# Edge stage of a graph network: message split by ScalarE, lists in pairs of tiles, a VectorE loop of 24 slots; routing marks shared with GpSimd

## What is computed

```python
h   = layernorm(x)
a   = concat(h[src], h[dst], edge_weight) @ mW1 + mb1        # 103125 edges
m   = layernorm(silu(a)) * ln_g + ln_b
msg = silu(m @ mW2 + mb2)
agg = segment_sum(msg, src, 3125)                            # sums by source node
x   = x + h + silu(concat(h, agg) @ uW1 + ub1) @ uW2 + ub2
# then: layernorm, a gelu network of width 1024 on the rows with the
# highest router scores, and the residual
```

## Time and profile before

| | |
|---|---|
| median of 3 runs | 2228.12 us (2223.9 to 2229.85) |
| the profiled execution, its own time | 2226.9 us |
| its span | 2225.2 us |
| PE busy | 1961.5 us (88%), 11037 matmuls |
| DVE busy | 1736.7 us (78%), 4578 instructions |
| ACT busy | 1303.2 us (59%), 2495 |
| POOL busy | 1238.9 us (56%), 1177 |
| mean granted clock of PE | 0.946 |

### The profile page before, as it was taken

The page is one execution under the profiler, slowest core; times in us unless marked ns, Lnnn a source line. Parts: engine busy times, 40 slices in busy tenths (PEclk is TensorE's granted clock), DMA queues, the critical chain, the costliest instruction groups (busy, mean ns, idle before and its releaser), DMA issues. The chain is left out here.

```text
span 2225.2 us, 45282 instructions
## 1 busy us (share of the span) xinstructions
PE 1961.5 (88%) x11037; PEld 1681.0 (76%) x11038; DVE 1736.7 (78%) x4578; ACT 1303.2 (59%) x2495; POOL 1238.9 (56%) x1177
## 2 busy tenths in 40 slices
PE   3546765379999999999999999999999999799996
PEld 2324554268888888888888888888888888677775
DVE  5899999678877877877878878778778778345895
ACT  1112331257777777777777777777777777423321
POOL 8753222376666666666667666666666665503000
PEclk9987777579999999999999999999999999899998
DMA  3000000344333333333333333333333333000001
GB/s 126 0 0 21 26 26 20 100 123 147 97 92 94 96 96 91 94 97 92 94 94 97 92 93 97 91 94 96 95 93 93 97 92 80 25 17 8 22 1 58
DMA packets 107787, 165.05 MB, mean 74 GB/s; under 512 B 42141, under 2 KB 78330, under 8 KB 107485
## 3 DMA queue, kind: packets, MB, share of 16 engines
q0 software_dynamic: 42016, 111.40, 18.4%
q1 hardware_dynamic: 59822, 47.94, 6.8%
q10 hardware_dynamic: 5900, 5.08, 0.7%
HBM read 152.30 MB, written 11.65 MB: 74 GB/s over the span
## 5 line engine op out<-in xcount | busy, mean ns | idle before, releaser
L907 POOL DMA_INDIRECT g_rows<-b_table,idx_ring x792 | 764.4, 965 | 439.7 <-ACT act L957 281.4
L1038 PE MATMUL ps<-w2g,nT 128*128 128x256 f32 x3336 | 789.3, 379 | 0.0
L1038 PEld LDWEIGHTS ps<-w2g,nT 128*128 128x128 f32 x3336 | 601.6, 190 | 64.6
L946 ACT ACTIVATE normed<-act,shift,rstd_e 128x255 f32<-128x255 f32 x834 | 449.6, 588 | 13.0 <-DVE shift L1105 9.5
L1021 PE MATMUL psG<-msg,ohf 128*125 128x256 f32 x1668 | 427.9, 379 | 0.1
L962 ACT ACTIVATE nT<-psM 128x512 f32<-128x512 f32 x417 | 248.9, 597 | 263.1 <-PE psM L1030 263.1
L1072 DVE TENSOR_TENSOR agg<-psG,agg 125x256 f32 x834 | 347.7, 417 | 67.6 <-issue 13.4
L1012 PE MATMUL psH<-a_sb,ohT 128*128 x1668 | 349.1, 332 | 26.4 <-DVE ohT L1125 24.7
L1136 DVE TENSOR_TENSOR g_rows<-psH,g_rows 128x512 f32<-128x512 f32 x417 | 284.7, 683 | 65.3 <-PE psH L1012 57.4
L1142 DVE BATCH_NORM_STATS2 stat_e<-act 128x6 f32<-128x256 f32 x834 | 310.2, 413 | 2.2 <-ACT act L957 2.2
L1021 PEld LDWEIGHTS psG<-msg,ohf 128*125 128x125 f32 x1668 | 284.4, 187 | 24.6 <-issue 0.3
(11 more groups left out here) (193 smaller groups left out, 1975.1 us busy)
## 6 DMA issues: line engine op xcount, KB each, us to landing
loc_rows<-loc_d SPq DMA_DIRECT2D x139, 187.5 KB
g_rows<-b_table,idx_ring POOLq DMA_INDIRECT x792, 2.8
h_sb<-in_x SPq DMA_DIRECT2D x1, 3125.0 KB
b_table<-b_out SPq DMA_DIRECT2D x25, 125.0 KB
x_all<-in_x ACTq DMA_DIRECT2D x1, 3125.0 KB
out<-x_all SPq DMA_DIRECT2D x5, 625.0 KB
ohT<-ew_d SPq DMA_DIRECT2D x139, 9.0 KB
idx_ring<-rec SPq DMA_DIRECT2D x132, 3.0 KB
```

Of the source, the lines that this page charges most:

```text
L907: pool.indirect_dma_start(g_rows[:, j, n, :], None, b_table[:, :], bass.IndirectOffsetOnAxis(ap=which, axis=0)).then_inc(s_gather[j], 16)
L946: ins = nc.scalar.activation(normed[:, j % 2, n, 0:D - 1], act1[:, (j - 10) % RING, n, 0:D - 1], ACT.Identity, scale=rstd_e[:, g % 2, k:k ...
L1038: mm = pe.matmul(ps2[:, k, n, :], nT[:, k, n, q, :], w2g[:, q, :], start=(q == 0), stop=(q == 1))
```

## The change

1. **Lists in pairs.** Each block's list is padded to whole pairs of tiles (256), so both tiles of a slot belong to one block: `PAIRS` is 429, `TILES` 858. There is one block number a pair (`pair_block`), and `reg_load` loads 6 registers a body on TensorE.
2. **One sum a slot.** `psG` gathers both tiles in one accumulation, so VectorE adds once a slot and no longer waits for an addition before it in the slot.
3. **The message is split.** ScalarE writes silu(`ps2`) once as `high`, float32r in SBUF, and, after `act1`, a second time in float32 in place in `ps2`. VectorE subtracts, `low` = `ps2` - `high`, float32r, as the last instruction of its slot. TensorE sums `high` and `low` with `ohf` in float32r: four products of one record each for two of two. `psG` now waits for `s_low`, which VectorE sets in the slot before, and so does `ps2` before it overwrites its buffer.
4. **VectorE's order and loop.** The shift moves from the slot's start to just before `g_rows`, variance 4 and 5 one step later; the hardware loop of VectorE alone has `SPAN` = 4 bodies of 6 slots and loads 24 registers at its start, 17 times. The written-out bodies keep 6 slots and load 6.
5. **Routing.** Of the 13 columns of `or_` VectorE makes 10 and GpSimd 3 (`pool_columns`), into four buffers `orp` in memory of `f1` and `f2`. GpSimd does the first four supers' columns before the chain of `jump`, and those of super s+4 after scatter s. `route(s)` waits for both (`s_or`, `s_orp`).

```diff
-TILES = (EDGES + BLOCKS * (WIN - 1 + P - 1)) // P
-TILES += TILES % 2
-PAIRS = TILES // 2
+PAIRS = (EDGES + BLOCKS * (WIN - 1 + 2 * P - 1)) // (2 * P)
+TILES = 2 * PAIRS
...
+                def pool_columns(s):
+                    if s >= PRING:
+                        pool.wait_ge(s_win, s - PRING + 1)
+                    for k in range(PCOLS):
+                        c = s * COLS + COLS - PCOLS + k
+                        ins = pool.tensor_scalar(orp[s % PRING][:, k, :], iota_n[:, :], r_all[:, c:c + 1], None,
+                                                 ALU.is_equal)
+                    ins.then_inc(s_orp, 1)
+
+                pool.wait_ge(s_places, 1)
+                for s in range(PRING):
+                    pool_columns(s)
...
                     pool.indirect_dma_start(rec_d[:, :], bass.IndirectOffsetOnAxis(ap=dest[:, s:s + 1], axis=0),
                                             recw[:, s % 4, :, :].rearrange("p w n -> p (w n)"), None).then_inc(s_scat, 16)
+                    if s + PRING < SUPERS:
+                        pool_columns(s + PRING)
...
                     pe.wait_ge(s_or, s + 1)
+                    pe.wait_ge(s_orp, s + 1)
...
-                    V.tensor_tensor(or_[:, s % 2, :, :], r_all[:, own].unsqueeze(2).broadcast_to([P, COLS, P]),
-                                    iota_v.unsqueeze(1).broadcast_to([P, COLS, P]), ALU.is_equal)
+                    mine = slice(s * COLS, (s + 1) * COLS - PCOLS)
+                    V.tensor_tensor(or_[:, s % 2, :, :],
+                                    r_all[:, mine].unsqueeze(2).broadcast_to([P, COLS - PCOLS, P]),
+                                    iota_v.unsqueeze(1).broadcast_to([P, COLS - PCOLS, P]), ALU.is_equal)
...
-                        nc.scalar.activation(msg[:, (j - 13) % 2, :, :], ps2[:, (j - 13) % 2, :, :], ACT.Silu).then_inc(s_msg, 1)
+                        nc.scalar.activation(high[:, (j - 13) % 2, :, :], ps2[:, (j - 13) % 2, :, :], ACT.Silu).then_inc(s_high, 1)
...
+                    if has(t, 13):
+                        act.wait_ge(s_high, t - 12)
+                        nc.scalar.activation(ps2[:, (j - 13) % 2, :, :], ps2[:, (j - 13) % 2, :, :], ACT.Silu).then_inc(s_msg, 1)
...
-                        pe.wait_ge(s_msg, t - 13)
+                        pe.wait_ge(s_low, t - 13)
                         pe.wait_ge(s_ohf, t - 13)
-                        need(pe, s_agg, 2 * t - 30)
+                        need(pe, s_agg, t - 15)
                         for n in range(2):
-                            mm = pe.matmul(psG[0:NB, k, n, :], ohf[:, k, n, :], msg[:, k, n, :], start=True, stop=True)
+                            pe.matmul(psG[0:NB, k, 0:D], ohf[:, k, n, :], high[:, k, n, :], start=(n == 0), stop=False)
+                            mm = pe.matmul(psG[0:NB, k, 0:D], ohf[:, k, n, :], low[:, k, n, :], start=False, stop=(n == 1))
...
+                    if has(t, 13):
+                        dve.wait_ge(s_msg, t - 12)
+                        V.tensor_tensor(low[:, (j - 13) % 2, :, :], ps2[:, (j - 13) % 2, :, :], high[:, (j - 13) % 2, :, :],
+                                        ALU.subtract).then_inc(s_low, 1)
+
+                def bodies(d, count):
+                    prepare(d, count)
+                    for i in range(count):
+                        for j in range(RING):
+                            slot((d + i) * RING + j, d + i, j, i)
...
-                with dve.Fori(PEEL, DG) as d:
-                    body(d)
+                with dve.Fori(0, (DG - PEEL) // SPAN) as e:
+                    bodies(e * SPAN + PEEL, SPAN)
```

More of the change, by code:

```diff
@@ L35 @@
 EQR = 4
+PCOLS = 3
+PRING = 4
 LAST = 15
 PEEL = 3
+SPAN = 4
 H = 1024
@@ L42 @@
 MAGIC = 12582912.0
+assert (DG - PEEL) % SPAN == 0 and PAIRS % 3 == 0
 assert NODES == NB * BLOCKS and 0 < TAIL <= EC and (COLS * P + BLOCKS * (WIN - 1)) // WIN <= P
-MAGIC_W, MAGIC_P = MAGIC * WIN, MAGIC * P
+MAGIC_W, MAGIC_P = MAGIC * WIN, MAGIC * 2 * P
 def build(nc, io):
@@ L145, in build @@
             k16 = sb("k16", [P, 1], F32)
[L146 to L150, removed]
+            tid = sb("tid", [P, PG], F32)
+            tb_c = sb("tb_c", [P, PG, BLOCKS], F32)
+            tb_f = sb("tb_f", [P, PG], F32)
+            tb_i = sb("tb_i", [P, PG], I32)
+            or_ = sb("or_", [P, 2, COLS - PCOLS, P], BF16)
+            orp = [half[:, k * PCOLS * P // 2:(k + 1) * PCOLS * P // 2].bitcast(BF16).rearrange("p (t r) -> p t r", t=PCOLS)
+                   for half in (f1, f2) for k in range(PRING // 2)]
             oqv = sb("oqv", [P, 2, COLS, PLANES, WIN], BF16)
@@ L594, in route @@
                     for t in range(COLS):
-                        mm = pe.matmul(psK[:, s % 3, 0:PLANES * WIN], or_[:, s % 2, t, :],
+                        marks = or_[:, s % 2, t, :] if t < COLS - PCOLS else orp[s % PRING][:, t - COLS + PCOLS, :]
+                        mm = pe.matmul(psK[:, s % 3, 0:PLANES * WIN], marks,
                                        oqv[:, s % 2, t, :, :].rearrange("p n w -> p (n w)"),
@@ L707, in _ @@
                 link(V.tensor_scalar(r_all[:, :], f2[:, :], 1.0 / WIN, None, ALU.mult))
[L708 removed]
+                V.tensor_tensor(q_all[:, :], place[:, :], f2[:, :], ALU.subtract).then_inc(s_places, 1)
+                dve.wait_ge(s_places, 1)
                 def flat(ap):
@@ L796, in build @@
             ohT = sb("ohT", [P, RING, 2, P], F32R)
-            ohf = sb("ohf", [P, 2, 2, NB], F32)
+            ohf = sb("ohf", [P, 2, 2, NB], F32R)
             g_rows = sb("g_rows", [P, RING, 2, D], F32)
@@ L801, in build @@
             nT = sb("nT", [P, 2, 2, 2, P], F32)
-            msg = sb("msg", [P, 2, 2, D], F32)
+            high = sb("high", [P, 2, 2, D], F32R)
+            low = sb("low", [P, 2, 2, D], F32R)
             var_e = sb("var_e", [P, 2, 6], F32)
@@ L1116, in slot @@
                     variance(t, d, j, 3)
-                    if has(t, LAST):
-                        add(t, j, 1)
-                    variance(t, d, j, 4)
                     if has(t, 1):
@@ L1126, in slot @@
                                         node_col[0:NB, 0:1], None, ALU.is_equal).then_inc(s_ohT, 1)
-                    variance(t, d, j, 5)
+                    variance(t, d, j, 4)
                     if has(t, 13):
@@ L1131, in slot @@
                                         ALU.is_equal).then_inc(s_ohf, 1)
+                    variance(t, d, j, 5)
+                    shifts(t, d, j)
                     if has(t, 2):
@@ L1144, in slot @@
                         ins.then_inc(s_bn, 1)
+                    if has(t, 13):
[7 more added lines that the diff above has]
+                            slot((d + i) * RING + j, d + i, j, i)
                 def body(d):
-                    prepare(d)
-                    for j in range(RING):
-                        slot(d * RING + j, d, j)
+                    bodies(d, 1)
                 V.tensor_copy(nodes, iota_n[:, 1:NB + 1]).then_inc(s_nodes, 1)
```

68 lines of the change are left out of this document (37 added, 31 removed).

## The result

| | before | after |
|---|---|---|
| median | 2227.01 us (2223.9 to 2229.85, 4 runs) | 2244.89 us (2243.95 to 2250.37, 4 runs) |
| profiled execution: span | 2225.2 us | 2242.1 us |
| mean granted clock of PE | 0.946 | 0.925 |

The change made the kernel **0.9% slower**: ratio 1.0086, 95% interval 1.0064 to 1.0107. Forecast were 2178 us and a range of 2092 to 2238. The time lies outside it, on the side of the rival "the longer body must be fetched anew, and the clock falls at each turn", which had a chance of 0.09 and was priced at 2255.

A forecast was written before the change was run, and what follows sets the result against it. TensorE was taken to bound the edge loop and VectorE the routing; -26 us for the edge loop, -22 for routing and -1 for the end, against 2226.9, gave 2178 us, range 2092 to 2238.

The forecast's parts named there:

- the longer body must be fetched anew, and the clock falls at each turn: Rival for VectorE's loop turn: code fetch and half clock make the kernel slower, slot 3.53, total 2255 us; chance 0.09.
- TensorE's pace: Edge loop: four fp32r sums take 0.48 us for 0.86, so a slot falls from 3.508 to 3.13 us.
- ScalarE and VectorE: Edge loop: ScalarE needs 2.96 to 3.0 us a slot, VectorE 2.94, both under TensorE's 3.13.
- The load of 24 registers: VectorE's loop turn: the load takes 5.46 us, twice that of 12 registers, once in 24 slots.
- VectorE is set back by 5.36: VectorE's loop turn: lateness from the 5.46 us load, plus 0.17, less 0.27 hidden by `low`.
- TensorE stops for 4.2: Edge loop turn: TensorE waits at psG for 5.36 less 1.15, 4.2 us, or 0.175 us a slot.
- The free lateness of 1.15: Edge loop: VectorE may run 1.15 us late before TensorE has to wait for `low`.
- The clock term: Edge loop: half speed after TensorE's stops was taken to cost 0.04 us a slot.
- Routing: Routing stage: ten columns instead of 13 on VectorE, three on GpSimd; -22 us over 62 supers.
- The end: End of the edge stage: slots shrink a little from last psH to last root, -1 us; node stage unchanged.

The follow-up runs named there:

- span1_fp32: Changed kernel with VectorE's loop at 6 slots and the message split undone (one silu, fp32 sums, no `low`): 2245.0 us, ratio 1.0083 to the kernel before.
- span1_b: Changed kernel with VectorE's loop at 6 slots, loading 6 registers: 2121.7 us, ratio 0.9529 to the kernel before; without _b, on the different chip, 2315.4 us.
- span2_load24_b: Changed kernel with VectorE's loop at 12 slots, loading 24 registers, 12 never used: 2324.5 us, ratio 1.0448; without _b, on the different chip, 2454.8 us.
- span3_b: Changed kernel with VectorE's loop at 18 slots, loading 18 registers, and five groups of 6 ahead of it instead of three: 2181.9 us, ratio 0.9808.
- span2_b: Changed kernel with VectorE's loop at 12 slots, loading 12 registers: 2155.9 us, ratio 0.9682 to the kernel before.
- span1_mix: Changed kernel with VectorE's loop at 6 slots, two columns on GpSimd, and marks of supers 2 and 3 behind the jump chain: 2120.4 us, ratio 0.9522.
- cols0: Changed kernel with all 13 routing columns back on VectorE, none on GpSimd: 2432.0 us on the different chip, 2258.05 us on another.

## Why the prediction was wrong, step by step

The forecast gave a turn 5.2 us of TensorE's time, 4.2 for the stop and 1.0 for the clock; it measured 9.4. Two terms failed: the fetch of the body, put at nothing, and the clock behind the stop, put at a third of what it took.

- **TensorE's pace: right.** 3.11 between turns for a forecast 3.13; fp32r sums at psH's price. span1_fp32 confirms the 0.4 us.
- **ScalarE and VectorE: right.** (That a write to PSUM costs no more was assumed without a row.) The Silu that writes PSUM lasts 0.59 us like its kin, and ScalarE needs 2.98 a slot (2.96 to 3.0 forecast). VectorE's 2.94 is met by the 2.9 that span1_b's 19.1 us leave.
- **The load of 24 registers: right.** 5.37 measured, 5.46 taken. The Trainium skill (Runtime: NRT & Kernel Launch, Instruction fetch mechanics) gave about 200 ns a register; 24 registers show 224 each here.
- **"VectorE is set back by 5.36": right for the load, and the step that failed.** The sum had no term for the code. The forecast put the fetch into a rival, because the old body of 120 instruction records never was fetched again; the new one has 445 (records from branch to branch). The fetch costs VectorE 2.6 us of standing a turn (8.07 for span2_load24_b's 5.47) and, with the clock, 9.4 - 7.0 = 2.4 us of TensorE's time. The Trainium skill's rule (same section: a taken branch to code outside the two pages that the engine holds waits for a fetch) pointed to it, and the traces agree in kind: 445 records are read anew each time round, 335 (span3_b) are not. Where between the two it begins no run shows. The weight given to it, 0.09, was the mistake; nothing in the trace of before spoke against it for a body four times as long.
- **"TensorE stops for 4.2": right for the case it described.** 3.9 without a fetch. With it, 6.2. But it was released by `ohT` first (2.6 of the 3.9) and by `low` second; the forecast had TensorE stop at psG for `low` alone, and it stops already at psH. The free lateness of 1.15 fits TensorE's idle time (0.2 and 3.9 us for turns of 1.28 and 5.47, so 1.1 to 1.6 is free), but a turn costs more than its idle time: 0.5 and 2.0 for turns of 1.28 and 2.81, as if only 0.8 were free.
- **The clock term: failed too.** Taken were 0.04 a slot, 1 us a turn, on the ground that the loop is dense. Stops of 3.9 us together in a dense loop brought half speed behind every turn and cost 2.7 us (span2_load24_b), in the changed kernel 3.0. The row that showed it stood in the prediction (3.69 us idle, then half speed) and was discounted. A stop of 1.5 us (span2_b) brought none.
- By estimate, neither error alone turns the sign. Without the fetch a turn of 24 slots at 7.0 us gives 3.11 + 0.29 = 3.40, and 2245 - 416 x 0.10 = 2203; with the fetch and the forecast's clock, 9.4 - 2.0 = 7.4 gives about 2210. Both together lose 1%.
- **Routing: right in kind, -13 for -22.** VectorE's super fell as forecast; its last `or_` comes 18.8 us earlier (388.50 for 407.26), not 24. But three marks take 1.78 and not 1.65, the scatter that follows 1.05, so GpSimd's super is 3.05 and not 2.6, and it catches up little when it is late: its last scatter starts 10.9 us behind VectorE's last `or_`, for 6.0 before. Twelve marks of 10.1 us ahead of the jumps put the first scatter 3.5 us later.
- **The end: -1 forecast, about -6 measured.** Last psH start to the span's end is 334.4 before and 328.4 after. The adds follow the last root as forecast, but the wait between them and the node stage fell from 8.99 to 2.45 us in every kernel with the new lists. What ends that wait isn't resolved; that it is fixed was an assumption. The node stage took 1.9 us more here (285.9 for 284.0).

The profiled spans add up: first psH 13.2 us earlier, from the first to the last psH 1492.5 us for 1456.5 (428 slots for 416), the end 6.0 shorter: +16.8 for the measured 16.9.

## What to carry to other kernels

Price the turn of a hardware loop as three things: the register load by its length, the fetch of a body that doesn't stay, and the clock behind the stop they cause; a longer loop spreads a turn thinner only as long as none of the three is new. Look in the trace for packets of instructions at the turns, and compare one engine's longest standstill with the lateness that its consumer can let pass: in 12 slots, two loads of 1.4 us cost 0.8, one of 2.7 costs 2.0, one of 5.4 costs 7.0. Here the loop of 12 slots with two loads of 6 registers keeps all that the split gives: 2118 us, 4.8% under the kernel before, with the loop of 6 and span1_mix within 0.2% of it.

## What was not expected of the hardware

- **One chip is different.** On it the kernel before took 2272 and 2278 us for 2225 to 2227 on the others, and the kernels with the new stage lost far more: span1 2315 for 2122, span2_load24 2455 for 2324, cols0 2432 for 2258. In its traces TensorE's counts arrive in bunches 0.06 us apart, up to 2.5 us late, while the granted clock is full. Whether TensorE itself or only its counts are held up, and why, stays open; no trace of the kernel before was taken there. On that chip even the best version is 1.8% slower than before, so a verdict from one chip can have the wrong sign.
- **A load of registers costs nearly the same for each register.** In the loop 6 take 1.41 us, 12 take 2.73, 18 take 4.05, 24 take 5.37: 235 to 224 ns each. Only the first load, of 6 outside the loop, is shorter, 1.0. VectorE stands for 1.28, 2.81, 4.1 and 5.47 us at such turns.
- **Code is read anew in small packets all along a long body**, and not only at its turn, but only the turn waits: with 445 records VectorE stands 2.6 us longer there, with 335 (span3_b) no fetch shows.
